# Gated attention on one Trainium2 core: four of eight head pairs as float32r passes with low parts by VectorE, and another order at the head of two stages

## What is computed

```
q = sum_e rw[t,e] * (x[t] @ Wq[e])        (k and v likewise, width 64)
attn = softmax(causal(q k^T / 8)) v       within each sequence of 64
out  = sum_e (attn * rw[t,e]) @ Wo[e]
```

## Time and profile before

| | |
|---|---|
| median of three runs | 3032.99 us |
| the profiled execution, its span | 3030.37 us, 3028.6 us |
| mean granted clock of TensorE | 0.98 |
| busy: PE (matmuls), DVE (VectorE) | 2886.0 us (95%), 2201.2 us (73%) |
| busy: ACT (ScalarE), POOL (GpSimd) | 1592.5 us (53%), 1176.9 us (39%) |
| DMA traffic | 212.25 MB, mean 70 GB/s |
| L2297, q/k products | 512 records, 248.0 us |
| L2539, weighting | 128 operations, 154.5 us |

### The profile page before, as it was taken

How to read it: one execution, slowest core, us unless ns; L and a number is a source line. 1 busy time by engine, 2 the same in 40 slices (tenths; PEclk the granted TensorE clock), 3 DMA queues, 4 the chain that set the end, 5 groups by cost and what they waited for, 6 DMA issues and landing times. The chain is left out here.

```text
span 3028.6 us, 90503 instructions
## 1 busy us (share of the span) xinstructions
PE 2886.0 (95%) x35122; PEld 2270.6 (75%) x35122; DVE 2201.2 (73%) x5731; ACT 1592.5 (53%) x2970; POOL 1176.9 (39%) x1244
## 2 busy tenths in 40 slices
PE   7999799999998999889997999999998999999978
PEld 6888545555556888757776888888887888888865
DVE  7777666666655666578887777778767777878866
ACT  6777311211213777667773333333336777777756
POOL 6777200000003777465540000000004677777754
PEclk9999899999999999989998999999998999999999
DMA  5000166666661000011112333333230000000001
GB/s 160 23 10 8 64 194 177 187 184 183 183 174 36 13 10 10 2 54 28 29 22 71 101 112 107 106 104 95 98 113 16 12 10 8 10 10 10 10 1 57
DMA packets 110876, 212.25 MB, mean 70 GB/s; under 512 B 18737, under 2 KB 30321, under 8 KB 110194
## 3 DMA queue, kind: packets, MB, share of 16 engines
q1 hardware_dynamic: 110194, 209.18, 23.5%
q10 hardware_dynamic: 512, 0.92, 0.1%
HBM read 198.49 MB, written 5.77 MB: 67 GB/s over the span
## 5 line engine op out<-in xcount | busy, mean ns | idle before, releaser
L384 PE MATMUL ps<-parts 128*128 128x512 f32 (+3 forms) x1568 | 622.5, 397 | 34.1 <-DVE parts L1002 18.1
L385 PE MATMUL ps<-parts 128*128 128x512 f32 (+3 forms) x1568 | 564.3, 360 | 0.0
L386 PE MATMUL ps<-parts 128*128 128x512 f32 (+3 forms) x1568 | 562.5, 359 | 0.0
L318 POOL TENSOR_TENSOR rstd<-mv,eps 128x4 f32<-128x4 f32 x106 | 21.2, 200 | 990.4 <-DVE mv L301 990.4
L1962 ACT ACTIVATE work<-ps 128x512 f32<-128x512 f32 x272 | 162.3, 597 | 443.0 <-PE ps L386 442.8
L384 PEld LDWEIGHTS ps<-parts 128*128 128x128 f32 (+2 forms) x1568 | 299.1, 191 | 106.8 <-ACT work L837 26.3
L582 POOL TENSOR_TENSOR work<-work 128x512 f32<-128x512 f32 x256 | 266.9, 1043 | 274.5 <-DVE work L972 274.5
L386 PEld LDWEIGHTS ps<-parts 128*128 128x128 f32 (+2 forms) x1568 | 298.1, 190 | 45.3
L385 PEld LDWEIGHTS ps<-parts 128*128 128x128 f32 (+2 forms) x1568 | 300.6, 192 | 20.2
L1927 PEld LDWEIGHTS ps<-early,work 128*128 128x128 f32 x2176 | 281.8, 192 | 18.7 <-DVE pause L2016 0.3
L1927 PE MATMUL ps<-early,work 128*128 128x128 f32 x2176 | 288.3, 276 | 0.1
(11 more groups left out here) (297 smaller groups left out, 6032.4 us busy)
## 6 DMA issues: line engine op xcount, KB each, us to landing
work<-gate_rows SPq DMA_DIRECT2D x128, 512.0 KB, 5.6
work<-expert_rows SPq DMA_DIRECT2D x512, 128.0 KB, 2.9
work<-gate_rows SPq DMA_DIRECT2D x128, 256.0 KB, 7.1
work<-in_ctxT SPq DMA_DIRECT2D x72, 192.0 KB, 2.4
out<-x SPq DMA_DIRECT2D x16, 256.0 KB, 2.3
work<-work SPq DMA_DIRECT2D x224, 16.0 KB
work<-work SPq DMA_DIRECT2D x16, 128.0 KB, 2.3
early<-in_l0f_w SPq DMA_DIRECT2D x1, 1536.0 KB
```

Source lines behind the costliest of these rows:

```text
L384: T.matmul(out, lh, rh, start=True, stop=False)
L385: T.matmul(out, lh, rl, start=False, stop=False)
L386: return T.matmul(out, ll, rh, start=False, stop=True)
```

## The change

In gated attention pairs 0, 1, 4 and 5 (`SPLIT`) are projected in float32r. VectorE weights such a pair in place in `wide`; ScalarE copies it into a float32r `high` buffer (`take_high`), VectorE subtracts (`take_low`), and TensorE does ten passes per pair: per expert three for q/k, and two for v, whose stationary tile holds the high and the low part of the weights side by side (their sums meet in the halves that `values` adds). The load that refills a `wide` buffer of a split pair waits for its low part. Pairs 2, 3, 6 and 7 stay float32, with two `hw` buffers in place of four. The weights are split once, high parts by ScalarE, low parts by GpSimd, at the head of the stage. In VectorE's turn low part 1 of group g+1 comes at s=0, 4 at s=2 ahead of the mask, 5 at s=4, and 0 of group g+2 at s=7. The heads of both stages are put in another order. `ex` shares `sm`'s memory, and the two product buffers lie where weights of the layer before were.

```
# experts: TensorE, then VectorE
+                if isinstance(g, int) and g == 0 and j == FIRST // P:
+                    te.wait_ge(w_low, 4)
...
-            te.wait_ge(w_low, 4)
...
+            mult(0, 0, 0), mult(0, 0, 1)
+            norm.take_moments(ve, 1)
             weights_low(1)
-            norm.vector(ve, 1)
-            block_of(0, 0, 0), block_of(0, 0, 1)
+            norm.scale(ve, 1)
+            weight(0, 0, 0), weight(0, 0, 1)
# gated_attention
+    SPLIT = (0, 1, 4, 5)
...
+                    if p in SPLIT:
+                        sp.wait_ge(low_ready, g * len(SPLIT) + (p - NW + 1 if p >= NW else p - 1))
...
+            def weights_low(i):
+                mine, theirs = slice(4 * i, 4 * i + 4), slice(8 * i, 8 * i + 4)
+                pool.wait_ge(w_high, 2 * i + 1)
+                G.tensor_tensor(wqk_low[:, mine, :], weights[:, theirs, 0:P], wqk_high[:, mine, :].bitcast(FP), ALU.subtract).then_inc(w_low, 1)
+                pool.wait_ge(w_high, 2 * i + 2)
+                G.tensor_tensor(wv_both[:, mine, DH:P], weights[:, theirs, P:QKV], wv_both[:, mine, 0:DH].bitcast(FP), ALU.subtract).then_inc(w_low, 1)
+
+            weights_low(0)
+            row_norms(0), weights_low(1)
...
+                if p in SPLIT:
+                    te.wait_ge(low_ready, g * len(SPLIT) + SPLIT.index(p) + 1)
+                    if p == 0:
+                        need(te, v2_out, g - 1)
+                    for e in range(2):
+                        x, head = 2 * SPLIT.index(p) + e, p == 0 and e == 0
+                        hi, lo = high[p % 2][:, e, :], low[p % 2][:, e, :]
+                        T.matmul(ps_q[u], wqk_high[:, x, :], hi, start=head, stop=False)
+                        T.matmul(ps_q[u], wqk_low[:, x, :], hi, start=False, stop=False)
+                        T.matmul(ps_q[u], wqk_high[:, x, :], lo, start=False, stop=False)
+                        T.matmul(ps_v[u], wv_both[:, x, :], hi, start=head, stop=False, skip_group_check=True)
+                        last = T.matmul(ps_v[u], wv_both[:, x, :], lo, start=False, stop=False, skip_group_check=True)
+                    last.then_inc(pair_done, 1)
+                    return
...
+            def take_high(g, p):
+                act.wait_ge(hw_ready, g * NP + p + 1)
...
+                A.activation(high[p % 2], wide[p % NW], ACT.Copy).then_inc(high_ready, 1)
...
                     take_values(g)
+                    if left(g + 1):
+                        take_high(g + 1, 4)
                     probs(g)
                     if left(g + 2):
                         gate_exp(g + 2)
+                    if left(g + 1):
+                        take_high(g + 1, 5)
                     take_probs(g)
                     if left(g + 2):
                         take_gates(g + 2, u)
+                        take_high(g + 2, 0), take_high(g + 2, 1)
...
+            def take_low(g, p):
+
+                ve.wait_ge(high_ready, g * len(SPLIT) + SPLIT.index(p) + 1)
+                V.tensor_tensor(low[p % 2], wide[p % NW], high[p % 2].bitcast(FP), ALU.subtract).then_inc(low_ready, 1)
...
-            for p in range(NHW):
-                weight(0, 0, p)
+            weight(0, 0, 0), weight(0, 0, 1), take_low(0, 0), weight(0, 0, 2), take_low(0, 1), weight(0, 0, 3)
             for part in range(11):
                 routing(1, 1, part)
+            weight(0, 0, 4), weight(0, 0, 5), take_low(0, 4), weight(0, 0, 6), take_low(0, 5)
             ve.wait_ge(n2_ready, 2 * TG)
-            norm.vector(ve, 2)
-            for p in range(NHW, NP):
-                weight(0, 0, p)
-            weight(1, 1, 0), weight(1, 1, 1)
+            norm.take_moments(ve, 2)
+            weight(0, 0, 7)
+            norm.scale(ve, 2)
+            weight(1, 1, 0), weight(1, 1, 1), take_low(1, 0)
...
+                        if s in (0, 4) and left(g + 1):
+                            take_low(g + 1, s + 1)
+                        if s == 2 and left(g + 1):
+                            take_low(g + 1, 4)
+                        if s == NP - 1 and left(g + 2):
+                            take_low(g + 2, 0)
```

More of the change, by code:

```diff
@@ L2163, in gated_attention @@
     n = c.ngroup
-    NP, NW, NHW, NM = NE0 // 2, 4, 4, 4
-    w = c.carve()
+    NP, NW, NM = NE0 // 2, 4, 4
+    SPLIT = (0, 1, 4, 5)
+    w, spent, r = c.carve(), c.carve(c.early[:, 0:4 * GT]), c.carve(c.parts)
     hn, hT = c.hn, [w([GT]) for _ in range(2)]
-    hw = [w([2, GT]) for _ in range(NHW)]
+    hw = [spent([2, GT]) for _ in range(2)]
+    high, low = [r([2, GT]) for _ in range(2)], [r([2, GT]) for _ in range(2)]
+    wqk_high, wqk_low, wv_both = r([NE0 // 2, P]), r([NE0 // 2, P]), r([NE0 // 2, P])
+    weights = c.w["l0f_w"].rearrange("p (e c) -> p e c", c=QKV)
     wide, split = [w([2, GT]) for _ in range(NW)], [w([2, GT]) for _ in range(NM)]
     qk, kT, v2, vd = w([GT]), w([GT]), w([GT]), w([TG, P])
-    sm, ex, pn, pT = w([TG, P]), w([TG, P]), w([TG, P]), w([TG, P])
+    sm, pn, pT = w([TG, P]), w([TG, P]), w([TG, P])
+    ex = sm
     mixed = [w([2, GT]) for _ in range(NM)]
@@ L2192, in gated_attention @@
         sem(s) for s in ("s", "s_read", "nmx", "exp", "rec", "p", "pt", "pt_out", "attn", "mixed", "y", "added"))
+    high_ready, low_ready, w_high, w_low = (sem(s) for s in ("high", "low", "w_high", "w_low"))
     LINKS = 18
@@ L2434, in take_probs, with weights_high @@
                 A.activation(pT.rearrange("p t q -> p (t q)"), ps_s, ACT.Copy).then_inc(pt_out, 1)
+            def weights_high(i):
+                mine, theirs = slice(4 * i, 4 * i + 4), slice(8 * i, 8 * i + 4)
+                A.activation(wqk_high[:, mine, :], weights[:, theirs, 0:P], ACT.Copy).then_inc(w_high, 1)
+                A.activation(wv_both[:, mine, 0:DH], weights[:, theirs, P:QKV], ACT.Copy).then_inc(w_high, 1)
+            def take_high(g, p):
+                act.wait_ge(hw_ready, g * NP + p + 1)
+                if not (isinstance(g, int) and g == 0 and p < NW):
+                    act.wait_ge(pair_done, g * NP + p - NW + 1 if p >= NW else g * NP - (NW - 1 - p))
+                A.activation(high[p % 2], wide[p % NW], ACT.Copy).then_inc(high_ready, 1)
+            weights_high(0)
             take_hT(0, 0), squares(0)
+            weights_high(1)
             act.wait_ge(freq_full, 1)
@@ L2536, in weight @@
                 ve.wait_ge(wide_in[p % NW], (g * (NP // NW) + (p // NW + 1)) * 16)
[L2537 to L2539 removed]
+                if p in SPLIT:
+                    V.tensor_tensor(wide[p % NW], bc(hT[u], 1, 2), wide[p % NW], ALU.mult).then_inc(hw_ready, 1)
+                    return
+                if not (isinstance(g, int) and g == 0 and p < NW):
+                    ve.wait_ge(pair_done, g * NP + p - NW + 1 if p >= NW else g * NP - (NW - 1 - p))
+                V.tensor_tensor(hw[p % 2], bc(hT[u], 1, 2), wide[p % NW], ALU.mult).then_inc(hw_ready, 1)
+            def take_low(g, p):
+                ve.wait_ge(high_ready, g * len(SPLIT) + SPLIT.index(p) + 1)
+                V.tensor_tensor(low[p % 2], wide[p % NW], high[p % 2].bitcast(FP), ALU.subtract).then_inc(low_ready, 1)
             def mix(g, i):
```

23 lines of the change are left out of this document (11 added, 12 removed).

## The result

After the change the kernel takes 3012.05 us (median of 4 runs, 3007.83 to 3016.57), against 3033.88 for the kernel before, run beside it (median of 4, 3032.87 to 3037.45). The ratio is 0.993, its 95% interval 0.9918 to 0.9943: some 22 us faster. Of all the executions told of here, one of the four of e10 took 3996.69 us at a mean granted clock of 0.65, and no ratio or stage time includes it. So the two traces differ by only 13.8 us, and I compare them stage by stage. A stage begins where VectorE sets its marks (L282).

A forecast was written before the change was run, and what follows sets the result against it. TensorE's own work was taken to bound gated attention. Loop and tail 24.6, less 1.7 at the stage's start, plus 1.3 in the experts, gave 24.2 us saved: 3009 us, range 3002 to 3020.

The forecast's parts named there:

- loop and tail: Gated attention: 1.7 us saved in each of 13 full turns, 1.8 in the last, 0.7 in the first, together 24.6.
- Price of a pair: TensorE in gated attention: ten passes take 2.38 us in place of 2.83, saving 0.45 per pair, 1.80 per turn.
- Gates to pair 0: Chain from gate rows through weightings to low part 0 arrives together with TensorE; a stall of 0.1 us per turn.
- Mask: VectorE's chain to low part 4 and TensorE's scores both end 11.5 us behind T0, the start of pair 0.
- Probabilities: From mask to normalised probabilities takes 5.2 us while TensorE has 5.85 of other work: slack 0.6, neither side changes.
- Buffers: Split pairs' buffers free later, so loads of pairs 6 and 7 come some 3 us later; cost nothing.
- First turn: First turn of the gated-attention loop saves an estimated 0.7 us of the 1.8, since low part 4 holds the mask.
- Start of the stage: Head of gated attention: 1.7 us lost to GpSimd's subtractions beside routing; pair 0 another 2.5 later, costing nothing net.
- Experts: New order at the experts' head runs the third block in TensorE's old gap: 1.3 us gained, bounds 0 and 2.5.
- Overrun: Rival: hand-offs between engines in gated attention lose 0.9 us more per turn, halving the gain, 3021 us; chance 0.2.
- Cheaper: Rival: a split pair's first pass also takes 0.23 us, saving 4.8 more, 3004 us; chance 0.08.
- VectorE as the bound: Rival: stretched low parts and weightings make the gate chain 2.2 us late per turn, slower kernel, 3054 us; chance 0.05.

The follow-up runs named there:

- e10: The same kernel as e4, the changed kernel with three reorderings together, measured again: 2999.85 us, ratio 0.9886 to the kernel before.
- e3: Changed kernel with VectorE's low part of pair 5 put ahead of the weighting of pair 6: 3007.16 us in one run.
- e4: Changed kernel with the three reorderings of e1, e2 and e3 together: 3002.65 us, ratio 0.9899 to the kernel before.
- e6: Changed kernel with VectorE making the low part of pair 0 twice in each turn: 3024.76 us.
- e7: Changed kernel with VectorE making the low part of pair 4 twice in each turn, ahead of the mask: 3027.72 us.
- e2: Changed kernel with GpSimd's second two weight subtractions moved behind the norm's power of group 1: 3013.61 us in one run.
- e5: Changed kernel with the head of the experts in its old order, gated attention left as changed: 3015.06 us in one run.
- e1: Changed kernel with ScalarE's copies for pairs 4 and 5 ahead of taking the second group's gates: 3006.09 us, ratio 0.9912 to the kernel before.
- e8: Kernel before the change, with the value products of a float32 pair ahead of its query/key products: 3028.98 us in one run.

## Why the prediction held, and where it did not

The forecast was 3009 us and 3012.05 came out, inside the range and on the side named. The sum, against the profiled execution, was 24.2 us; the two stages gave 22.1. That nearness is in part luck: it hides three errors that partly cancel, and the first row hides two more.

| step | forecast | measured |
|---|---|---|
| loop and tail (13 full turns, first, last) | 24.6 | 27.0 |
| head of the stage | -1.7 | -7.2 (-3.7 to -5.3 in the other four traces of this head) |
| experts | +1.3 | +2.3 |

**Price of a pair: right from its first to its last start, 0.17 short for its neighbours.** The passes are 0.23 us apart and the first takes 0.31, so a split pair is 2.39. But the 2.83 of a float32 pair leaves out the 0.1 that it costs its successor, and the 2.38 of a split one leaves out that it starts 0.08 sooner behind the work ahead. A full turn without waits is 33.29 (e3, e4): 2.47 shorter, not 1.80, which is 0.62 for each of four pairs in place of 0.45. Against this stand waits of 0.56 per turn in place of 0.1. So a turn saved 1.91 where 1.7 was forecast, by two errors of about half a microsecond with opposite signs. The Trainium skill's gap for an isolated matmul of 512 columns (TensorE: Matmul & The Clock Gate, Back-to-back issue gap: 216 ns, and 131 for a sustained stream of weight loads and matmuls) is below what the trace shows for these passes, 0.23; the measurement decided here.

**Gates to pair 0: the chain right, the stall too small.** The low part ends 0.2 before TensorE starts the pair in the turn shown, and e6 shows that the slack is nil. But as the pairs are cheaper than forecast, TensorE comes sooner: where no other wait holds it back, in e3, it waits 0.39 per turn here and not 0.1. In after the waits before pair 5 hide most of that. **Mask: right** to 0.2 us (T0 + 11.3 where 11.5 was forecast, the end of TensorE's scores T0 + 11.2 where 11.5 was forecast), routing starts at T0 + 5.75 (forecast 5.8), and GpSimd's first operation of the row norms took 1.43 beside a weighting. **Probabilities: right**, 0.5 of slack where 0.6 was forecast; e7 finds 0.3.

**Buffers: wrong.** The prediction had the late loads of pairs 6 and 7 "cost nothing", covered until T0 + 16. The load of pair 6 is late in nine of the twelve full turns. It does not stop TensorE by itself; VectorE waits for it, and the low part of pair 5 waits behind. e3 puts this at 3.3 us against after, and at 4.7 between the means of all loops with either order. The prediction asked when a load is needed, and not what is queued behind the instruction that waits for it.

**First turn: mis-sized.** It saved 0.1 us (31.99 to 31.91), not 0.7: TensorE waited 1.08 there for the probabilities, since the mask came late, and 0.72 at pair 5.

**Start of the stage: the step that failed.** Its first term held: 1.7 was forecast for GpSimd's subtractions beside the routing, and 1.1 measured. Its second, pair 0 later by 2.5, held too: 11.31 - 8.38 = 2.9. What failed is the "nothing" for what follows. The four cheap pairs and the less float32 work at half clock were to give the 2.5 back, but the step looked at pairs 0 and 1 only and did not read ScalarE's queue for pair 4. There a copy stood behind a taking that waits for TensorE: 2.97 us idle in each of the six traces with that order, and behind it a stretch of half clock that cost 3 us in this trace and in e2, 1.7 in three others and nothing in e5. The 5.5 us by which the head missed the forecast hold that chance part; in the other four traces it missed by 2.0 to 3.6. e1, with that one order changed, has 26.77 us from pair 0 to the doubled values against 29.55 before, and e4 and e10 have 26.14 and 25.85: 2.8 to 3.7 given back against the 2.9 that pair 0 came later. With that order the "nothing" of the prediction holds.

**The lock.** In the head the routing step with two inputs (L2531) took 0.95 us in place of 0.23 beside GpSimd's subtraction, and ended 0.08 after it; the next, with one, took 0.62 in place of 0.20 and ended 0.06 after the second subtraction. In e2 they were 0.23 and 0.20 again. In the experts GpSimd's root took 1.76 and 2.53 in place of 0.20 and 1.01, and its first part ended 0.1 behind VectorE's first long subtraction. The Trainium skill (SBUF — State Buffer, SBUF: two separate sides) says, of a VectorE operation with two SBUF inputs and a GpSimd operation that reads SBUF, that the one that starts first holds the shared ports for its whole instruction and the other is blocked; this trace agrees. By that rule the head could have lost 2.0 us; it lost 1.1, since the two routing steps came 0.4 and 0.2 us after the subtractions had begun and would have taken 0.2 each in any case. (The VectorE operations of the earlier trace rows from which the prediction took its 1.6 ran beside GpSimd operations of 96x512 and 96x256, not of 128x512.)

**Experts: right in mechanism, a microsecond too small.** The root did wait for both long subtractions, as the sum took it, and the norm was scaled 20.2 us into the stage where the forecast's 1626.3 means 20.6. The gain at the fourth block was 2.0 us as forecast. The 0.8 taken off for half clock showed in part: at the block behind it 1.7 of the 2.0 were left in this trace, and 0.3 to 1.9 in the other eight with this order. The stage ended 2.3 earlier, 2.1 in the mean of all traces.

**The rivals.** Overrun fell: the waits are 0.56 us per turn, where the forecast had 0.1 and this rival 0.9 more. Cheaper, by a first pass of 0.23, fell as a mechanism: the first pass stays at 0.31 or more wherever float32 work stands ahead of it. But the 0.08 per pair that it named is there all the same, ahead of the first pass and not behind it; the waits took it back. VectorE as the bound fell for this change, but e6 and e7 show how near it is: one subtraction more in a turn cost 14 and 17 us, although VectorE is idle for a fifth of the time.

## What to carry to other kernels

Price a pass by what it does to the instruction behind it as well as by its own length: read the starts of the work ahead and behind in both surroundings. Look for short waits in the steps, since the idle time of the profile leaves them out where records overlap. Where a split adds hand-offs between engines, walk every queue once for the first turn of the loop as for the middle one. In each queue ask what stands behind an instruction that waits (for a transfer, or for the engine that is to be fed): here two such orders cost some 3 to 6 and 3 to 5 us, and each was mended by changing the place of one or two operations. A gain or a loss of a few microseconds in one part is to be compared with every trace in which that part is the same.

## What the runs showed that was not expected

- The first product behind the side-by-side value products (64 columns each) takes 0.1 us more than behind others: eight products of 128x128 took 0.99 there against 0.88, and a query/key product 0.53 against 0.43 (e8).
- The first pass of a split pair starts 0.03 us behind the start of the 128x128 product ahead, where a float32 product starts 0.11 behind it.
- The same wait of 2.97 us on TensorE was followed by 6.2, 5.8, 3.4, 3.4, 3.4 and no us at a granted clock of 0.50 in six traces, which cost from nothing to as much again as the wait.
- Operations of 128x4 on GpSimd took 1.43 and 1.76 us beside long VectorE operations with two inputs, in place of 0.20, and 2.53 in place of 1.01.
- A subtraction of 1.14 us, added on an engine that is busy for four fifths of a turn, lengthened the turn by 1.29 us at one place and by 0.92 at another.
- Stages that are instruction for instruction the same took up to 4 us more or less from one execution to the next, and one head took 52.4 to 56.0, so a difference of one stage is read from that stage, and a difference of two single executions tells little under that.
